# Moving the experts' first loads into the last attention steps, and the split of the row maxima from VectorE to GpSimd

## What is computed

```
xn = layernorm(x)                          # x: 4 x 1024 x 256
out = x + attention(xn) + experts(xn)

attention: q, k, v = xn @ Wq, xn @ Wk, xn @ Wv      # 16 heads of 16
    scores = causal(q k^T) + alibi bias, / sqrt(16)
    w = softmax(scores); ctx = w @ v; ctx @ Wo + bo

experts: logits = rmsnorm(xn) * scale @ router      # 8 experts, best 2 of each token
    a token's row goes through its two experts:
    gate, up = row @ Wgate[e], row @ Wup[e];  y = (gelu(gate) * up) @ Wdown[e]
    experts(xn) = sum over the two of weight * expert_scale[e] * y
```

## Time and profile before

| | |
|---|---|
| median of three runs | 880.79 us |
| the profiled execution | 878.63 us, of it 876.8 us span |
| PE busy | 801.6 us (91%) |
| DVE busy | 580.4 us (66%) |
| ACT busy | 484.0 us (55%) |
| POOL busy | 407.5 us (46%) |
| attention, from 112 to 586 us: exponentials (L825) | 576 of 602 ns |
| maxima (L664) | 512 of 754 ns |
| masks (L644) | 128 of 636 ns |

### The profile page before, as it was taken

The page is one execution under the profiler, slowest core; times in us unless marked ns, Lnnn a source line. Parts: engine busy times, 40 slices in busy tenths (PEclk is TensorE's granted clock), DMA queues, the critical chain, the costliest instruction groups (busy, mean ns, idle before and its releaser), DMA issues. The chain is left out here.

```text
span 876.8 us, 18100 instructions
## 1 busy us (share of the span) xinstructions
PE 801.6 (91%) x6338; PEld 489.4 (56%) x6338; DVE 580.4 (66%) x1560; ACT 484.0 (55%) x1011; POOL 407.5 (46%) x478
## 2 busy tenths in 40 slices
PE   4999968999998999999999999856999999999597
PEld 2555513344433444444444444326999999999497
DVE  4766479999999988888888888202333334333387
ACT  1444402777777677777777777852333333333474
POOL 6666400112111253344543442214677777775497
PEclk9999956999999999999999999996999999999799
DMA  8899775875346645776557700009322223222585
GB/s 192 277 281 283 251 111 70 103 86 73 51 53 86 76 76 81 105 86 100 83 82 97 87 25 3 6 2 330 113 93 95 92 93 95 91 92 73 154 258 179
DMA packets 93649, 100.51 MB, mean 115 GB/s; under 512 B 32700, under 2 KB 74300, under 8 KB 93500
## 3 DMA queue, kind: packets, MB, share of 16 engines
q1 hardware_dynamic: 84600, 80.40, 46.7%
q0 software_dynamic: 8960, 18.95, 6.9%
HBM read 63.89 MB, written 35.00 MB: 113 GB/s over the span
## 5 line engine op out<-in xcount | busy, mean ns | idle before, releaser
L825 ACT ACTIVATE probs<-spsum 128x512 f32<-128x512 f32 x576 | 317.5, 602 | 145.6 <-PE spsum L898 138.8
L664 DVE CUSTOM_DVE_ANT_0 junk<-mpsum,mask 128x128 bf16<-128x128 f32 (+7 forms) x512 | 359.2, 754 | 45.7 <-issue 30.0
L872 PE MATMUL mpsum<-ks,qs 102*128 102x512 bf16 (+3 forms) x768 | 184.3, 344 | 28.5 <-DVE maxima L664 22.0
L898 PE MATMUL spsum<-qs,ks 105*128 105x512 bf16 (+3 forms) x768 | 198.4, 330 | 4.8 <-ACT probs L825 3.4
L644 POOL TENSOR_SCALAR_AFFINE_SELECT probs<-probs 128x512 f32<-128x512 f32 x128 | 79.0, 636 | 253.3 <-ACT probs L825 253.0
L918 PE MATMUL cpsum<-probs,vs 128*17 128x256 f32 (+2 forms) x2560 | 154.0, 361 | 1.5 <-POOL probs L644 0.8
L1091 PEld LDWEIGHTS gu<-xTs,w_now 128*128 128x128 f32 x1152 | 142.2, 195 | 4.6 <-issue 1.0
L1091 PE MATMUL gu<-xTs,w_now 128*128 128x128 f32 x1152 | 142.9, 278 | 0.3 <-issue 0.3
L872 PEld LDWEIGHTS mpsum<-ks,qs 102*128 102x128 bf16 x768 | 67.7, 100 | 111.8 <-DVE maxima L664 55.1
L898 PEld LDWEIGHTS spsum<-qs,ks 105*128 105x128 bf16 x768 | 67.1, 97 | 91.0 <-ACT probs L825 39.7
L918 PEld LDWEIGHTS cpsum<-probs,vs 128*17 128x17 f32 x2560 | 59.0, 96 | 82.2 <-issue 37.5
(11 more groups left out here) (119 smaller groups left out, 657.9 us busy)
## 6 DMA issues: line engine op xcount, KB each, us to landing
qk_parts<-ctxT SPq DMA_DIRECT2D x32, 384.0 KB, 3.7
qs<-qk_parts SPq DMA_DIRECT2D x96, 128.0 KB, 5.7
ks<-qk_parts SPq DMA_DIRECT2D x96, 128.0 KB, 6.2
yk<-expert_rows SPq DMA_DIRECT2D x32, 256.0 KB, 3.1
v_rows<-ctxT SPq DMA_DIRECT2D x8, 544.0 KB, 3.6
vs<-v_rows SPq DMA_DIRECT2D x16, 272.0 KB, 10.8
ctxT<-in_x SPq DMA_DIRECT2D x8, 512.0 KB, 6.2
xn_rows<-ctxT SPq DMA_DIRECT2D x8, 512.0 KB, 5.7
```

The costliest lines, as they stand in the source:

```text
L664: last = dve.tensor_tensor_reduce(junk[:, slot, c:c + w], mpsum[:, slot, c:c + w], keep["mask"][:, S - w:S], 1.0, 3 * NEG, ALU.add, ALU.ma ...
L825: act.activation(probs[:, u % PRING, h], spsum[:, SCORE_AT["S", n, h] % SRING], ACT.Exp, scale=SCALE).then_inc(exp_done, 1)
L872: last = pe.matmul(mpsum[:, slot, at + c:at + e], qs[hq][0:R_MAX, h, qt * P:(qt + 1) * P], ks[hq][0:R_MAX, h, c:e], start=True, stop=True)
L898: last = pe.matmul(spsum[:, SCORE_AT["S", n, h] % SRING, c:c + w], ks[hq][:, h, kt * P:(kt + 1) * P], qs[hq][:, h, q0:q0 + w], start=True, ...
```

## The change

- The q and k tensors of the four head groups become one tensor `stacks`. The down weights, the ring of gathered rows and the ring of results y lie in the part of head groups 0 and 1, the x rows in that of groups 2 and 3. Buffers of `combine` lie over the same and over `w_gu`.
- SyncE loads the down weights in quad 13, and the map (`places`) in quad 14. GpSimd issues the first six gathers in quad 15, behind unit 5. In `experts` both are gone.
- The split of the maxima is done before they are turned: GpSimd does five small operations on 128 x 32 behind the mask of unit 6 (`split_maxima`), into three bf16 parts beside each other in `msplit`. TensorE turns all three by one bf16 matmul with an identity (96 x 128), and ScalarE copies the outcome to `mparts` (`turned`), behind the exponential of unit 7, head 0. VectorE has no part in it.
- T moves from pair 11 to pair 12, in the first quad from behind item 0 of the next to behind item 1.

```diff
-    out[first + 1].insert(0, (1, NI - 1))
+    out[first + 2].insert(0, (1, NI - 1))

+def gather_rows(pool, scratch, keep, s):
+    pool.indirect_dma_start(keep["rows"][:, s % RR], None, scratch["xn"],
+                            bass.IndirectOffsetOnAxis(ap=keep["places"][:, s, 0:1].bitcast(U32), axis=0)).then_inc(keep["rows_in"][s % RR], 16)

 # attend, SyncE
             def maxima_rows(n, hq):
-                sp.wait_ge(max_split, n + 1)
+                sp.wait_ge(t_taken, n + 1)
                 sp.dma_start(qs[hq][R_MAX:ROWS, :, :], mparts[:, hq % 2, :]).then_inc(mrow_in[hq], 16)
...
+                if t == B * NQ - 3:
+                    sp.wait_ge(pv_done, PRING + NU * t)
+                    for e in range(NE):
+                        sp.dma_start(keep["w_down"][:, e * DH:(e + 1) * DH], ins["w_down"][:, e * DH:(e + 1) * DH]).then_inc(keep["w_down_in"], 16)
                 if has(1):
                     maxima_rows(t + 1, (hq + 1) % NQ)
+                if t == B * NQ - 2:
+                    sp.wait_ge(entries_out, 16 * 2 * NT)
+                    sp.dma_start(keep["places"]..., scratch["map"]...).then_inc(keep["places_in"], 16)
...
-            sp.wait_ge(entries_out, 16 * 2 * NT)
-            sp.dma_start(keep["places"]..., scratch["map"]...).then_inc(keep["places_in"], 16)

 # attend, GpSimd
                     mask_unit(NU * t + j, j % NU)
+                    if (t, j) == FIRST_ROWS:                    # (15, 5)
+                        wait_apart(pool, pv_done, PRING + NU * (B * NQ - 2))
+                        wait_apart(pool, keep["places_in"], 16)
+                        for s in range(AHEAD):                  # 6
+                            gather_rows(pool, scratch, keep, s)
+                    if j == T_UNIT - 1 and has(1):              # 6
+                        split_maxima(t + 1)
                     if j in MAP_UNITS and t >= MAP_FROM:
                         map_entries(...)
+            def split_maxima(t):
+                top = maxima[:, t % 2].rearrange("p h q -> p (h q)")
+                wait_apart(pool, m_taken, ITEM_NO[t, NI - 2] + 1 + RING)
+                if t > 0:
+                    pool.wait_ge(t_ready, t)
+                pool.tensor_scalar(msplit[:, 0], top, -1.0, None, ALU.mult).then_inc(max_step, 1)
+                pool.wait_ge(max_step, 4 * t + 1)
+                pool.tensor_tensor(mrest[:, :], top, msplit[:, 0], ALU.add).then_inc(max_step, 1)
+                pool.wait_ge(max_step, 4 * t + 2)
+                pool.tensor_scalar(msplit[:, 1], mrest[:, :], -1.0, None, ALU.mult).then_inc(max_step, 1)
+                pool.wait_ge(max_step, 4 * t + 3)
+                pool.tensor_tensor(mrest[:, :], mrest[:, :], msplit[:, 1], ALU.add).then_inc(max_step, 1)
+                pool.wait_ge(max_step, 4 * t + 4)
+                pool.tensor_scalar(msplit[:, 2], mrest[:, :], -1.0, None, ALU.mult).then_inc(max_split, 1)
+            pool.tensor_scalar(ident_b[:, :], keep["ident"][:, :], 1.0, None, ALU.mult).then_inc(ident_set, 1)

 # attend, VectorE: the branch of item NI - 1 (L667 to L680) is gone

 # attend, ScalarE
+            def turned(t):
+                act.wait_ge(t_ready, t + 1)
+                act.activation(mparts[:, t % 2, :], spsum[0:12 * KT, SCORE_AT["T", t] % SRING, 0:P], ACT.Copy).then_inc(t_taken, 1)
...
                             exp(n, u, h)
+                            if (j, h) == (T_UNIT, T_HEAD) and has(1):    # (7, 0)
+                                turned(t + 1)

 # attend, TensorE
                     score_buffer("T", t)
-                    pe.wait_ge(m_taken, ITEM_NO[t, NI - 2] + 1 + RING)
-                    pe.transpose(spsum[0:4 * KT, SCORE_AT["T", t] % SRING, 0:P], maxima[:, hq % 2]..., keep["ident"][:, :]).then_inc(t_ready, 1)
+                    pe.wait_ge(max_split, t + 1)
+                    pe.matmul(spsum[0:12 * KT, SCORE_AT["T", t] % SRING, 0:P], msplit..., ident_b[:, :],
+                              start=True, stop=True).then_inc(t_ready, 1)

 # experts
-            for e in range(NE):
-                sp.dma_start(w_down[:, e * DH:(e + 1) * DH], ins["w_down"][:, e * DH:(e + 1) * DH]).then_inc(w_in, 16)
...
-            pool.wait_ge(places_in, 16)
-            for s in range(AHEAD):
-                gather(s)
```

More of the change, by code:

```diff
@@ L90 @@
 SRING = 3
+RR = 8
+AHEAD = 6
+FIRST_ROWS = (B * NQ - 1, 5)
 PAIRS = 2 * NU
@@ L130, in item_orders @@
 def item_orders():
-    seq = [(0, k) for k in range(NI - 1)] + [(1, 0), (0, NI - 1)] + [(1, k) for k in range(1, LEAD)]
+    seq = [(0, k) for k in range(NI - 1)] + [(1, 0), (1, 1), (0, NI - 1)] + [(1, k) for k in range(2, LEAD)]
     for t in range(B * NQ):
@@ L157, with head_buffers @@
 SCORE_SEQ, SCORE_AT = score_slots()
-def head_buffers(nc, ctx):
+T_UNIT, T_HEAD = next((n, h) for (_, n, h), after in zip(SCORE_SEQ[1:], SCORE_SEQ[2:]) if after == ("T", 1))
+def head_buffers(nc, ctx, stacks):
     sb = lambda name, shape, dt=F32: ctx.enter_context(nc.sbuf_tensor(name, shape, dt))
@@ L614, in _ @@
             steps(sp, body)
-            sp.wait_ge(entries_out, 16 * 2 * NT)
-            sp.dma_start(keep["places"][:, :, :].rearrange("p s c -> p (s c)"), scratch["map"].rearrange("(p s) c -> p (s c)", p=P)).then_inc(keep["places_in"], 16)
         @block.gpsimd
@@ L797, in _ @@
                 item(0, 0, k)
-            item(1, 1, 0)
-            item(0, 0, NI - 1)
-            for k in range(1, LEAD):
+            for k in range(LEAD):
                 item(1, 1, k)
@@ L807, in body @@
                     for j, k in PAIR_ITEMS[p]:
-                        if has(j):
+                        if has(j) and k < NI - 1:
                             item(t + j, (hq + j) % NQ, k)
@@ L968, in experts @@
         w_gu = keep["w_gu"]
-        w_down = sb("w_down", [P, NE * DH, D])
-        rows = sb("rows", [P, RR, D])
-        places, places_in = keep["places"], keep["places_in"]
+        w_down, rows, y, places = keep["w_down"], keep["rows"], keep["y"], keep["places"]
+        w_in, rows_in = keep["w_down_in"], keep["rows_in"]
         xT = sb("xTs", [P, 2, DH, P])
@@ L979, in experts @@
         yp = ctx.enter_context(nc.psum_tensor("yp", [P, 2, CH], F32))
-        w_in = sem("w_in")
-        rows_in = [sem(f"rows_in{i}") for i in range(RR)]
         y_out = [sem(f"y_out{i}") for i in range(RR)]
@@ L1005, in gather @@
                     pool.wait_ge(tp_ready, s - RR + 1)
-                pool.indirect_dma_start(rows[:, s % RR], None, scratch["xn"],
-                                        bass.IndirectOffsetOnAxis(ap=places[:, s, 0:1].bitcast(U32), axis=0)).then_inc(rows_in[s % RR], 16)
+                gather_rows(pool, scratch, keep, s)
             def scatter(s):
```

90 lines of the change are left out of this document (45 added, 45 removed).

## The result

The changed kernel takes 855.39 us (median; 854.89 to 856.15), the kernel before 880.73 beside it (879.84 to 881.36): a ratio of 0.9723, interval [0.971, 0.9737]. The forecast was 860.8 with a range from 856.5 to 869.5. The sign was right, and each part of the change gave something where it was forecast to. In two of the five groups of runs further down every kernel took some 30 us more, and one execution in experiment 5 took 1031.09 us at a mean granted clock of 0.742 where its fellows had 0.964 to 0.966, so ratios are compared within a group only and that execution is left out.

The account below looks back on a forecast made before the run. TensorE paces later quads, VectorE early ones; only the gathers hold the experts back. 8.2 + 6.0 + 0.8 + 5.2 − 0.2 = 20.0 us gained, so 860.8 against the 880.79 median; range 856.5 to 869.5, chance 0.81.

Parts of the forecast that it names:

- The hand-over: Attention to experts: with gathers moved ahead, first gate matmul waits only for `w_now`, at 592.6 instead of 600.78: 8.2 us gained.
- keeps its spacing: Experts behind the first gate matmul: same spacing as before, clock again at 0.50, slow first tiles not won back.
- T1 to T5: Early quads, paced by VectorE: the split's hold of 1.40 us goes, 1.2 each taken, 6.0 us gained, ends 4 and 7.
- T6: Quad with the last routing steps, then steady: 0.8 us gained from the split leaving VectorE.
- T7 to T14: Eight later quads: 0.86 us of VectorE's hold less 0.2 for a new exponential wait, 0.65 each, 5.2 us; ends 0.4 and 0.86.
- T0: First quad, T one item later and the copy behind it: counted zero, ends −0.5 and +0.9 us lost.
- T15: VectorE has nothing behind the split there: nothing gained; in quad 14 ScalarE's copy adds 0.2 to 0.3 us.
- GpSimd's chain: Split's five operations on GpSimd: 1.9 us, done 0.6 before T wants it; far end 4.1 us, 1.6 late.
- Rivals 1 and 2: GpSimd's chain ends late, TensorE waits: 872 us, chance 0.10; every GpSimd operation waits out a VectorE maximum: near 930, 0.03.
- Rival 3: Hand-over gives little: tiles wait for something of the new block, TensorE starting at 594 instead of 591; 864 us, chance 0.05.
- rival 4: In attention VectorE isn't what holds TensorE after T; the 0.86 us reappears as another wait; near 869 us, chance 0.08.
- the first wait: Sign in attention: row "PE mpsum waits for DVE maxima" falls from 15.6 to 5 us or less.

Follow-up runs that it names:

- experiment 5: Kernel after with two more operations of 0.29 us in GpSimd's chain: 861.53 us, 0.9793; in a slowed group 890.37, 0.9832.
- second pair: Both kernels profiled once more, unaltered (before_b, after_b); the rerun of the kernel after measured 855.27 us, 0.9719.
- experiment 2: Kernel after with the loads of the down weights and the six gathers back in `experts`, behind attention: 863.61 us, 0.9814.
- experiment 4: Kernel before with T one pair later, split still on VectorE, layout of after, map read in quad 14: 875.14 us, 0.9935; slowed group 900.97, 0.9943.
- Experiment 8: Kernel after with the first tile's weights copied in attention: 888.89 us, 0.9764 (slowed group); with seven gathers too: 888.48, 0.9757 there, undisturbed 852.25, 0.9694.
- experiment 3: Kernel after with T back in pair 11, the split still on GpSimd: 884.63 us, 1.0058.

## Why the forecast was right or wrong

**The hand-over (8.2; it gave 7.74, and 8.90 in the second pair of profiles).** Right in its chain: no gather on it, `w_now` last, the first gate matmul at 6.6 instead of 14.3. The block opened later than assumed: TensorE starts 4.73 us after attention's last copy ends (570.17 to 574.90), where I had put 591.0, 4.6 after 586.44, and VectorE copies from 5.76 after it, where the rows of before gave 591.71 − 586.44 = 5.27. That is the missing half microsecond. The 1.2 us between the two pairs lie in before, where the first gathered rows come at different times.

Of what follows I wrote "keeps its spacing" and "not won back", and no run speaks against it. In the first pair the clock does look better: it is granted at 0.50, the lower of its two levels, until 606.3 in before, 5.5 us into the gate matmuls, and until 580.5 in after, 3.7 us into them, and from the first tile's gate matmuls to the third's it takes 7.59 us and 6.72. But the same stretch takes 6.27 in the other profile of before and 6.29 to 7.42 in five of after, so the difference isn't shown to be the change's. It is the same with the gathers: the sixth tile's gate matmuls start 4.04 us behind the fifth's in after and 3.44 in before (an undisturbed step is 2.87), but two kernels that gather behind attention have 4.00 and 3.96, with the same wait (experiments 2 and 4; the row is experiment 2's):

```profile
600.45 0.44 PE L1103 MATMUL tp<-ident,stacks 128*128 128x128 f32 x2 [0.87 <-DMA stacks<-xn_rows,places]
```

Experiment 8 takes that wait away.

**T1 to T5 (6.0; 7.05) and T6 (0.8; 0.70).** By the distances of the `ctxT` copies they gave 1.42, 1.10, 1.52, 1.50 and 1.51. The hold of 1.40 a quad was read rightly; the discount to 1.2 for new waits of TensorE is what failed, since T's place gave as much as they took: by experiment 4 the place brings 0.9 of the five quads' 7.0, GpSimd 6.1, which is 1.2 a quad.

**T7 to T14 (5.2; 6.91).** Each gave 0.86 instead of 0.65. The step that failed: I priced the hold at 0.86, the new wait for an exponential at −0.2, and T's leaving pair 11 at nothing. The new wait came (514.59, 0.36 by its row, and 1.96 − 1.31 = 0.65 over that stretch). But in pair 11 the transpose and a wait for the exponential behind it had cost another 0.21, which is won. The price was in the rows I had: a mirror image of the 0.2 that I did charge. Experiment 4 says more: the later place by itself, with the split still on VectorE, brings 0.56 of the 0.87, and GpSimd adds 0.31. Why VectorE's hold costs TensorE less one pair later wasn't tested beyond the rows there. And without the place GpSimd's split loses (experiment 3). So my reasoning had the cause as VectorE's operations, with the order as a small cost; in these quads neither part gives the 0.87 without the other, and the order alone gives the larger share. In the quads with routing it is the operations.

**T0 (zero; 1.1, and 0.3 in the second pair) and T15 (−0.2; 0.0).** T came later, and the rows are issued at the same time as before, 26.71 us from the start of attention instead of 26.73, but the first score stands at 29.60 instead of 30.39 (142.26 and 143.57 on the profiles' clocks). So the rows were there sooner behind their issue; why isn't shown. With the place alone they are issued at 27.96 and this quad loses (experiment 4). The bound I had set was too narrow on this side: "−0.5 and +0.9 lost" allowed a gain of half a microsecond.

**GpSimd's chain (1.9; 1.71).** Right within 0.2: 0.29 and 0.245 us an operation against 0.28 and 0.26; the sum's 1.9 also held 0.17 for the start. The Trainium skill's rule of the port pair ("SBUF — State Buffer", "Who interferes with whom") did not bite: eleven ns lie between the shortest and the longest of the sixteen of L671, though VectorE took maxima beside most of them. By that page's exemption for one SBUF input, the trace agrees. Rivals 1 and 2 fell with these rows; what a late chain costs is experiment 5, 0.4 us a late quad for 0.74 more in the chain. Rival 3 fell with TensorE's start at 574.90, rival 4 with the fall of the first wait from 15.6 to 3.5.

**The range.** Its low end was a gain of 23.6, with hand-over 8.8, T1 to T5 7, T6 0.9 and the late quads 6.9. Attention's two large terms came out at exactly these best values (7.05 and 6.91), the hand-over below (7.74): 22.4 with T6. The other 2.4 of the 24.8 come from where I had put zero: T0 1.1, the projections and the opening of `combine` 0.5 each, the experts 0.3. Of these the opening of `combine` is the change's: it takes 6.2 to 6.3 us in every kernel that gathers early and 6.8 in every one that gathers late; why wasn't looked into. The projections and the experts differ by as much between two profiles of before (113.18 and 112.65, 210.7 and 209.5), so that part is luck, as it is how often the slow start of `combine` falls on either kernel. A range that takes only the sum's named terms to their ends leaves no room for stages that were said not to change.

## What to carry to other kernels

When an operation leaves a slot in a hand-written order, price the slot it leaves by the same rows as the slot it enters; the wait that is charged at one is won at the other. A step that is moved to another engine and to another place should be tried in its four combinations, since here GpSimd's split without T's new place made the kernel slower, and T's place without it gave the larger part of the late quads' gain. A small operation that one engine's queue holds up is worth more on an idle engine than its duration says, as long as it ends before its reader comes: here the room was some 0.4 us in a quad of 26, and hardly any in most quads with routing. A stage's difference is worth no more than what the same kernel shows between two profiles: here up to 1.2 us at the hand-over, 1.3 in the first tiles and 2.5 in `combine`.

## What the hardware showed unexpectedly

In the two slowed groups the additional time came on two chips, of which one also ran an undisturbed group. It stood where indirect DMAs are issued: in the experts (228 to 236 us instead of 211), in quads 5 to 12 (some 0.8 to 1.1 us each), and for the kernels with early gathers in the last quad. In the last quad of the kernel after, TensorE and ScalarE stopped together while the gathers ran, for nothing the profile names, and the clock fell behind that stop:

```profile
568.55 0.60 ACT L860 ACTIVATE probs<-spsum 128x512 f32<-128x512 f32 x1 [3.25 <-remote]
569.20 0.61 PE L938 MATMUL spsum<-stacks 105*128 105x512 bf16 x1 [2.75 <-issue]
```

```profile
565.00:570.00 5.00, 2.25 (x24) 0.59 (x16) 0.00 (x0) 0.98 (x3) 2.84 (x3) 0.84 0.36 105
570.00:575.00 5.00, 5.00 (x36) 1.23 (x28) 0.00 (x0) 3.56 (x7) 0.00 (x0) 0.50 0.00 0
```

From the last but one `ctxT` copy to the last it took 20.02 us instead of 15.17; kernels that gather late kept their 15.2 there in these groups. What was behind it was not found; the early gathers are then not free, and the ratio there was 0.9773 instead of 0.972.

The start of `combine` runs longer at the low clock in some profiles than in others of the same kernel: 58.5 or 60.7 us for the same instructions. In before the granted clock from 824 to 830 us is 0.94 in the one and 0.58 in the other.
